# Ratio attention: ScalarE normalises the tiles, and x joins the output's accumulation through a product with the unit matrix

## The reference

```python
def _layernorm(x, axis=-1, eps=1e-05):
    m = jnp.mean(x, axis=axis, keepdims=True)
    v = jnp.var(x, axis=axis, keepdims=True)
    return (x - m) / jnp.sqrt(v + eps)
...
    x = x + _L0_attn_ref(_layernorm(x, axis=-1), L0_attn_w_qkv, L0_attn_b_qkv, L0_attn_w_out, L0_attn_b_out)
```

## Time and profile before

| | |
|---|---|
| median of 3 runs | 784.0 us (782.09 to 784.91) |
| the profiled execution's own time | 782.49 us |
| its span (first to last instruction) | 780.7 us |
| mean granted TensorE clock | 0.938 of full |
| busy share of the span: PE, PEld, DVE, ACT, POOL | 84%, 64%, 64%, 46%, 40% |

### The profile page before, as it was taken

How to read it: one execution, slowest core, us unless ns; L and a number is a source line. 1 busy time by engine, 2 the same in 40 slices (tenths; PEclk the granted TensorE clock), 3 DMA queues, 4 the chain that set the end, 5 groups by cost and what they waited for, 6 DMA issues and landing times. The chain is left out here.

```text
span 780.7 us, 16875 instructions
## 1 busy us (share of the span) xinstructions
PE 659.7 (84%) x6081; PEld 502.5 (64%) x6081; DVE 496.9 (64%) x1365; ACT 359.7 (46%) x976; POOL 311.6 (40%) x445
## 2 busy tenths in 40 slices
PE   4999999999999877744993699978998884999990
PEld 3768777877877766643441587657776662677770
DVE  3677776776776789857368873556886786333330
ACT  1445454545545566734375753434655541223220
POOL 2244545555552377731000020233745533455641
PEclk9999999999999999976997799998999996999996
DMA  9632323222220000007500134609101021234334
GB/s 276 218 75 62 78 60 78 76 66 72 65 55 2 2 3 3 3 1 229 230 2 0 68 155 170 258 3 406 68 3 61 2 83 54 42 65 67 60 47 67
DMA packets 31697, 65.08 MB, mean 83 GB/s; under 512 B 5792, under 2 KB 21792, under 8 KB 29312
## 3 DMA queue, kind: packets, MB, share of 16 engines
q1 hardware_dynamic: 26016, 55.73, 21.7%
q0 software_dynamic: 4688, 7.18, 5.8%
q10 hardware_dynamic: 912, 1.10, 0.5%
HBM read 57.67 MB, written 7.37 MB: 83 GB/s over the span
## 5 line engine op out<-in xcount | busy, mean ns | idle before, releaser
L487 ACT ACTIVATE prob<-s_sb,negm 128x257 f32<-128x257 f32 x128 | 66.2, 517 | 94.2 <-DVE negm L710 94.2
L424 POOL TENSOR_SCALAR bias<-dist,cst 128x257 f32<-128x257 f32 x128 | 59.8, 486 | 97.8 <-DVE dist L697 88.0
L706 DVE CUSTOM_DVE_ANT_0 s_sb<-psum,bias 128x257 f32<-128x257 f32 x128 | 49.4, 423 | 51.5 <-PE psum L567 48.2
L545 PE MATMUL psum<-ctxT,shared 128*128 128x257 f32 x256 | 62.9, 389 | 1.7 <-DMA msk<-in_mask 1.7
L553 PE MATMUL psum<-shared,ctxT 128*128 128x256 f32 x256 | 60.4, 379 | 0.0
L2616 PE MATMUL psum<-ex_w,shared 128*128 x184 | 58.3, 460 | 0.6 <-ACT shared L2509 0.6
L1706 POOL TENSOR_TENSOR wn<-wn,cst 128x1 f32<-128x1 f32 x8 | 4.7, 588 | 123.9 <-DVE wn L1833 123.9
L553 PEld LDWEIGHTS psum<-shared,ctxT 128*128 128x128 f32 x256 | 48.4, 189 | 6.8
L545 PEld LDWEIGHTS psum<-ctxT,shared 128*128 128x128 f32 x256 | 47.2, 195 | 8.0 <-issue 2.4
L567 PE MATMUL psum<-kT,qbd 64*128 64x257 f32 x256 | 48.6, 429 | 2.7 <-DVE mx L706 2.5
L2616 PEld LDWEIGHTS psum<-ex_w,shared 128*128 128x128 f32 x184 | 33.1, 190 | 15.4 <-issue 0.8
(11 more groups left out here) (349 smaller groups left out, 1656.5 us busy)
## 6 DMA issues: line engine op xcount, KB each, us to landing
ctxT<-in_ctx_T SPq DMA_DIRECT2D x32, 257.0 KB
ex_w<-in_w SPq DMA_DIRECT2D x1, 5632.0 KB, 17.3
kpos<-in_kpos SPq DMA_DIRECT2D x32, 128.5 KB
msk<-in_mask SPq DMA_DIRECT2D x32, 128.5 KB
near_turned<-in_ctx_T_tiles SPq DMA_DIRECT2D x4, 1028.0 KB
ff_used_up<-in_ctx_T_tiles SPq DMA_DIRECT2D x4, 1028.0 KB
near_rows<-in_ctx_tiles SPq DMA_DIRECT2D x4, 1024.0 KB, 7.5
ff_used_up<-in_ctx_tiles SPq DMA_DIRECT2D x4, 1024.0 KB, 7.2
```

Source lines behind the costliest of these rows:

```text
L424: nc.gpsimd.tensor_scalar(bias[n % 2][:, g, :], dist[n % 2][:], c.slope[:, g:g + 1], 1.0, ALU.mult, ALU.mult).then_inc(bias_ready, 1)
L487: nc.scalar.activation(prob[n % 2][:, g, :], s_sb[n % 2][:, g, :], ACT.Exp, bias=negm[:, b, g:g + 1], accum_out=esum[t % 2][:, b, g:g + 1]) \
L545: ins = nc.tensor.matmul(kv[m][:, 0:SK], w["xa_k"][:, k, P * m:P * m + P], ctxT[n % BT][:, k, :], start=(k == 0), stop=(k == KT - 1))
L706: nc.vector.tensor_tensor_reduce(s_sb[n % 2][:, g, :], sc[g % 2][:, 0:SK], bias[n % 2][:, g, :], 1.0, float("-inf"), ALU.add, ALU.max, mx[ ...
```

## The change

ScalarE takes two pieces of work from VectorE. The normalisation of tiles 2 to 7 becomes one ACTIVATE of form Identity, `xn = rstd * x + below`, at the end of ACT's step; it needs `below = -mean * rstd`, which a new GpSimd instruction of one column (`shift`) computes after the root. And the sum `x + y` is no longer made by VectorE: PE first multiplies `x[:, n, :]` with the unit matrix into the output's bank, adds the output projection to it in PSUM, and ACT copies the finished sum into x (`act_output`), one step earlier in the pipeline than DVE did it. The three pieces run in both blocks.

```diff
+        def shift(pool, n):
+            pool.wait_ge(rstd_ready, n + 1)
+            nc.gpsimd.tensor_scalar(below[n % 2][:], mv[n % 2][:, 0:1], rstd[n % 2][:], -1.0, ALU.mult, ALU.mult) \
+                .then_inc(below_ready, 1)
...
             if there(u + 4):
                 root(pool, u + 4)
+                shift(pool, u + 4)
...
+        def act_norm(act, n):
+            act.wait_ge(below_ready, n - 1)
+            act.wait_ge(xn_ready, n)
+            at_least(act, xT_full, n - 1)
+            nc.scalar.activation(xn[n % 2][:], x[:, n, :], ACT.Identity, bias=below[n % 2][:], scale=rstd[n % 2][:]) \
+                .then_inc(xn_ready, 1)
+
+        def act_output(act, n):
+            act.wait_ge(y_full, n + 1)
+            nc.scalar.copy(x[:, n, :], y_bank[:, 0:D]).then_inc(y_done, 1)
...
+            if there(u + 4) and u + 4 >= 2:
+                act_norm(act, u + 4)
+            if there(u - 1):
+                act_output(act, u - 1)
...
         def pe_output(pe, n):
+            at_least(pe, y_done, n)
+            pe.wait_ge(bias_added, n + 1)
+            nc.tensor.matmul(y_bank[:, 0:D], c.ident, x[:, n, :], start=True, stop=False, skip_group_check=True)
             pe.wait_ge(oT_ready, n + 1)
-            at_least(pe, y_done, n)
-            project_tokens(nc, y_bank, oT[n % 2], w["ra_o"]).then_inc(y_full, 1)
+            for k in range(KT):
+                ins = nc.tensor.matmul(y_bank[:, 0:D], oT[n % 2][:, k, :], w["ra_o"][:, k, :], start=False,
+                                       stop=(k == KT - 1), skip_group_check=True)
+            ins.then_inc(y_full, 1)
...
-            if there(u - 2):
-                dve_output(dve, u - 2)
             if there(u):
                 off_maximum(dve, u)
-            if there(u + 4):
-                norm_apply(dve, u + 4)
...
             ratio.act_exp(act, NT - 1)
+            ratio.act_output(act, NT - 2)
             ratio.act_own(act, NT - 1)
             turned_weights(6, 3)
+            ratio.act_output(act, NT - 1)
...
-            ratio.dve_output(dve, NT - 2)
             ratio.dve_features(dve, NT - 1)
             normed(0, 0, FIRST)
-            ratio.dve_output(dve, NT - 1)
             dve.wait_ge(ratio.y_done, NT)
```

More of the change, by code:

```diff
@@ L994, in __init__ @@
         s_banks, x_bank, qk_bank, v_bank, o_banks, y_bank = psum[:, 0:2, :], *bank[4:7], psum[:, 2:4, :], bank[7]
-        eps = sb("eps", [P, 1])
+        eps, below = sb("eps", [P, 1]), [sb(f"below{i}", [P, 1]) for i in range(2)]
         st = Steps(sem("dve_steps"))
+        below_ready = sem("below_ready")
         consts_set, marked, row_full, row_ready = sem("consts_set"), sem("marked"), sem("row_full"), sem("row_ready")
@@ L1200, in dve_row @@
             nc.vector.tensor_tensor(row[:], qk_bank[:, 0:D], w["ra_bo"][:], ALU.add).then_inc(row_ready, 1)
[L1202 to L1205, removed]
         def dve_step(dve, u):
@@ L1230, in __init__ @@
         self.act_own, self.act_exp, self.pe_output, self.pe_values = act_own, act_exp, pe_output, pe_values
-        self.dve_features, self.dve_output = features, dve_output
+        self.dve_features, self.act_output = features, act_output
         self.xT_done, self.qk_done, self.v_done, self.s_read, self.o_full = xT_done, qk_done, v_done, s_read, o_full
```

## The result

| | before | after |
|---|---|---|
| median, 8 executions each on one chip | 783.56 us (782.04 to 785.27) | 779.23 us (778.17 to 781.57) |
| ratio | | 0.9952, 95% interval 0.9937 to 0.9968 |
| the profiled execution's own time | 782.49 us | 781.57 us |
| its span, its mean granted clock | 780.7 us, 0.938 | 779.8 us, 0.936 |

The changed kernel is faster by 0.48%, or 3.8 us; the forecast was 4.0. The profiled execution, though, is only 0.9 us shorter than that of before. Both are so: the medians are taken over many executions, and the profiled one of the changed kernel happened to be the slowest of its eight.

The account below looks back on a forecast made before the run. The prediction took a cycle over DVE, POOL and ACT as the bound, not PE. Four steps at 0.90 us plus 0.46 at the seam gave 4.0 us, from 782.49 to 778.5, median 780.0; range 777.7 to 784.2.

Parts of the forecast that it names:

- The cycle over DVE, POOL and ACT: In the steps: reciprocal, quotient, mask, maximum, subtraction, exponential and denominators over three engines set the 9.80 us step, PE doesn't.
- 0.90 us in each of four steps, 3.6 in all: From subtraction L1188 to the next reciprocal: 2.91 us become 2.01, with 0.62 from the subtraction and 0.27 from the normalisation.
- The shift, 0.3 us: New one-column POOL instruction between root and L879, taken as 0.3 us; it lets L1188 take 0.69 us instead of 1.31.
- The seam, 0.46 us: At the passage to the feed-forward, the last two tiles' statistics start at about 357.93 instead of 358.39: 0.46 us gained.
- L1205 in the steps is worth nothing: Taking L1205 (0.42 us) off DVE gains nothing in the first block's steps; it only adds to the wait for POOL's mask.
- ACT keeps about 1 us before the exponential: ACT's two new instructions cost 0.96 us at most and the step shortens by 0.9, leaving about 1 us idle.
- PE's cover is used up in a slow-clock step: The unit-matrix product uses up PE's wait before L923 in a slow-clock step; L923 comes some tenths late, scores keep over 2 us.
- Rival A: L879 gets in before the subtraction on the ports: 1.70 us subtraction, 0.11 us lost a step, median 784.0; chance 20%.
- Rival C: PE's lower clock makes it the bound: one step at that level turns the gain into a loss, median 786; chance 6%.
- Rival B: The four steps go partly one way, partly the other, or ACT is late in some: 2 us gained, median 782; 12%.
- The rule on the ports: DVE and GpSimd share SBUF ports; when a two-input DVE instruction contends with GpSimd, the first issued holds them to its end.
- The total, 4.0 us: Whole kernel: 4 x 0.90 + 0.46 = 4.0 us, profiled execution from 782.49 to 778.5 us, median 780.0.

Follow-up runs that it names:

- e1: The changed kernel with the shift moved behind L879 on GpSimd; first four steps 9.52 to 9.55 us, ratio to before 0.9995.
- e4: The changed kernel with the normalisation given back to VectorE and no shift; steps 9.77 to 9.81 us, seam 2.06 us, ratio to before 0.9997.
- e8: The changed kernel with the product with the unit matrix made three times; steps 8.90 to 8.93 us, one execution of 778.93 us.
- e7: The changed kernel with the shift behind L879 and, in its old place, a like instruction without the wait; subtraction 1.55 us, steps 9.76 to 9.79 us.
- e2: The kernel before with only the shift added behind the root on GpSimd, its result unused; steps 9.16 to 9.19 us, ratio to before 0.9994.
- e11: The kernel before, unchanged, run again for a second profile; 93.42 us from first reciprocal to first rounding, against 94.04 in the first profile.
- e12: The kernel of e2, unchanged, run again for a second profile; 91.67 us from first reciprocal to first rounding, against 90.93 in e2.
- e9: The changed kernel with the second cross attention's folded-weight products moved ahead of the spreading of H's top; ratio to before 0.9954.

## Why the prediction was right, point by point

- *The cycle over DVE, POOL and ACT sets the step, PE doesn't.* Shown: the steps follow the subtraction and the normalisation alone (e1 to e4), and three unit products change nothing (e8).
- *0.90 us in each of four steps, 3.6 in all.* Measured 0.86 to 0.89, by the distances of the reciprocals 9.78, 9.81, 9.79, 9.80 less 8.91, 8.92, 8.93, 8.91: 3.51 us. Its two parts, 0.62 and 0.27, were measured apart as 0.62 and 0.25.
- *The shift, 0.3 us.* It takes 0.26 or 0.27. The order of events by the hundredth was as forecast, root + 0.64 for its start and root + 0.79 for the subtraction. The sentence that a shift of 0.21 us would do the same was too sure: by these rows L879 would have been issued at about root + 0.81 (an estimate), 0.02 us behind the subtraction.
- *The seam, 0.46 us.* 2.52 to 2.06 us, shown by e4 too. What was not foreseen is that the seam ahead of it varies: PE's 24 turned weights (L1419) took 5.15 us in the first profile of before, 4.40 in the second and 5.36 in the changed kernel's, so that from last reciprocal to first rounding only 0.23 us show between the first two (27.77 and 27.54). Against the second profile of the kernel before (27.14) the changed kernel is 0.40 us longer there. The 0.46 us are shown at their place, then, and not in the stretch around it.
- *L1205 in the steps is worth nothing.* Shown by e4. The wait for the mask grew from 0.37 to 0.68 us instead.
- *ACT keeps about 1 us before the exponential.* Right: the forecast was worked out from a step with the slower clock, and in such a step 1.16 us were left; in one with the faster clock 1.9, where the kernel before had 2.9. Two errors of the sum nearly cancel: the two instructions cost 0.75 us and not 0.96, since they overlap with their neighbours, and ACT's wait for PE's projection L856, which the sum left out, grew from 0.38 to 0.60 us.
- *PE's cover is used up in a slow-clock step.* So it came, by 0.28 us, at no cost.
- *Rival A* did not happen, but e7 produced it by taking 0.09 us away: a subtraction of 1.55 us where I had priced 1.70, and steps of 9.78 us in place of 9.90. That A stayed away hung on 0.07 us, with a shift whose length no row had shown; in this the forecast was lucky. *Rival C* did not happen. *Rival B* is not seen in any profile.
- *The rule on the ports* (the Trainium skill, "SBUF — State Buffer", "Who interferes with whom"): the trace agrees, in both directions. Whichever was issued first, L879 or the subtraction, ran to its end, 0.04 us of difference in e7 and 0.07 in the changed kernel, and the other waited: 1.55 us in place of 0.69, or 1.52 in place of 1.04.
- *The total, 4.0 us.* Measured 3.8. The mechanism and its size in the steps are shown; that the total agrees so closely is partly luck, since some tenths were lost ahead of the stage, the seam's gain can't be seen around it, and the changed kernel had the higher clock more often: at like clock it gains 3.3 us.

Open: why the kernels draw the lower clock so unequally often. The level in three places (the turned weights, the large products, the fold) differs between profiles by about 3 us in all, and one profile a run tells it for that execution alone. At the higher clock e1 is 0.8 us faster than the kernel before where 1.6 were expected, and e4 isn't faster at all; the time lost ahead of the stage is about of that size, but this is an argument and no run shows it.

## What to carry to other kernels

Where DVE and POOL each have a queue of SBUF work, the order of their issues within a tenth of a microsecond decides who waits, and the one that can afford it should be second: an instruction moved, or even added, on the engine with time to spare can be worth more than one taken from the bound engine. Read an instruction's duration against its shortest: 1.31 against 0.69 us said that more was to be had from the subtraction than from the normalisation behind it. And compare a stage between marks inside it; the total of one profiled execution here showed 0.9 us of a gain of 3.8. Where totals are compared, set executions of like granted clock beside each other: e2's total showed 0.5 us of a gain of 1.5 to 2.9.

## What the runs showed of the hardware

- An added GpSimd instruction of 0.26 us made each step 0.62 us shorter (e2), and the same form in the same place took all of it back when it had no wait on a semaphore and so started 0.54 us behind the root's start, not 0.64 (e7).
- The same program meets the clock at 1.00 or 0.96, and at 0.70 or 0.50, in the same stretches of two executions (e11), and the two stretches differ by 1.2 us each. How often an execution has the lower mean clock differs by kernel: 18 of 64 before, 11 of 13 with one short GpSimd instruction more (e2, e12), none of 14 changed.
- PE's idle time before a group of products is not a gap to be filled at the full rate: the first fold (28 records) took 7.7 us at the lower level in a gap of 5.4 (e9).
